# Third layer's attention: the mask added to the scores by VectorE on the way to SBUF, in place of a 16-bit product with a diagonal matrix

## The reference

```python
q = einsum('btd,dnh->btnh', layernorm(x), Wq) + bq
k = einsum('bsd,dnh->bsnh', ctx, Wk) + bk
v = einsum('bsd,dnh->bsnh', ctx, Wv) + bv
scores = einsum('bsnh,btnh->bnts', k, q) * (1.0 / sqrt(64.0))
adder = (1.0 - attention_mask[:, None, :, :]) * -10000.0
probs = softmax(scores + adder, axis=-1)
x = x + tanh(g_xattn[2]) * (einsum('bnts,bsnh->btnh', probs, v) @ Wo + bo)
```

## Time and profile before

| | |
|---|---|
| time, median of 3 runs | 1793.32 us (1789.34 to 1793.98) |
| the profiled execution's own time | 1796.88 us |
| its span, first to last instruction | 1795.2 us |
| mean granted TensorE clock over the span | 0.872 |
| busy over the span | PE 1370.8 us (76%), DVE 975.7 (54%), ACT 686.4 (38%), POOL 361.9 (20%) |
| this attention's loop, about | 719 to 1062 us of the span |

### The profile page before, as it was taken

One profiled execution on the slowest core, in us unless ns is written; L12 is line 12 of the kernel. 1 busy time (PEld: TensorE's weight loads), 2 busy tenths in 40 slices (PEclk: granted clock), 3 DMA queues, 4 the chain that ended last, 5 costly groups with the idle time before them and its releaser, 6 DMA issues. The chain is left out here.

```text
span 1795.2 us, 32731 instructions
## 1 busy us (share of the span) xinstructions
PE 1370.8 (76%) x10700; PEld 1157.7 (64%) x10709; DVE 975.7 (54%) x2389; ACT 686.4 (38%) x1370; POOL 361.9 (20%) x452
## 2 busy tenths in 40 slices
PE   4999657749599993999999989999999951102554
PEld 3777535649599982788888878799999840102232
DVE  3777654627512215555555547423223736988786
ACT  2555443510244431333333333355554252302454
POOL 1000000001122210222222222366665300001000
PEclk9999967869599996999999988799999986556787
DMA  3000020770211106111111010122223324020001
GB/s 95 19 18 13 11 76 1 231 218 1 76 40 38 38 21 210 45 45 44 48 47 51 8 58 26 42 91 92 92 90 109 141 62 109 9 56 1 1 0 47
DMA packets 96891, 108.63 MB, mean 61 GB/s; under 512 B 27888, under 2 KB 83952, under 8 KB 96496
## 3 DMA queue, kind: packets, MB, share of 16 engines
q1 hardware_dynamic: 83168, 77.77, 14.4%
q0 software_dynamic: 9984, 27.28, 4.9%
q10 hardware_dynamic: 3664, 2.63, 0.5%
HBM read 85.55 MB, written 20.97 MB: 59 GB/s over the span
## 5 line engine op out<-in xcount | busy, mean ns | idle before, releaser
L3474 PEld LDWEIGHTS L2f_bank<-L2f_xT,L2f_w_tile 128*128 128x128 f32 x1280 | 156.1, 193 | 7.5 <-ACT L2f_xT L3534 3.5
L3474 PE MATMUL L2f_bank<-L2f_xT,L2f_w_tile 128*128 128x128 f32 x1280 | 156.9, 276 | 3.0 <-ACT L2f_xT L3534 3.0
L759 POOL TENSOR_TENSOR L2x_probs<-L2x_probs,L2x_inv_sum 128x512 f32<-128x512 f32 x64 | 65.2, 1040 | 289.4 <-DVE L2x_inv_sum L1026 289.4
L3583 DVE TENSOR_TENSOR L2f_hT<-L2f_gate_h,L2f_bank 128x256 f32<-128x256 f32 x80 | 33.7, 421 | 151.9 <-ACT L2f_gate_h L3541 151.9
L3528 ACT COPY L2f_w_tile<-L2f_w_up 128x1024 f32 x80 | 83.7, 1046 | 34.8 <-issue 34.8
L3474 PEld LDWEIGHTS L1f_bank<-L1f_xT,L1f_w_tile 128*128 128x128 f32 x768 | 90.7, 194 | 1.1
L3474 PE MATMUL L1f_bank<-L1f_xT,L1f_w_tile 128*128 128x128 f32 x768 | 90.9, 277 | 0.0
L3399 POOL DMA_INDIRECT L2f_y_rows<-L2f_xn,L2f_put_row x80 | 79.0, 987 | 56.2 <-DVE L2f_xn L3599 52.7
L3391 POOL DMA_INDIRECT L2f_rows<-L2f_x_rows,L2f_take_row x80 | 77.8, 972 | 45.3 <-DVE L2f_take_row L3374 21.6
L1008 DVE TENSOR_REDUCE L2x_top<-L2x_bank 128x4 f32<-128x512 f32 x64 | 43.9, 686 | 78.8 <-PE L2x_bank L828 78.8
L3491 PE MATMUL L1f_bank<-L1f_w_down,L1f_hT 128*128 x384 | 86.7, 379 | 0.0
(11 more groups left out here) (649 smaller groups left out, 3340.5 us busy)
## 6 DMA issues: line engine op xcount, KB each, us to landing
L1f_w_up<-in_L_ffn_w SPq DMA_DIRECT2D x16, 512.0 KB, 9.6
L1f_w_down<-in_L_ffn_w SPq DMA_DIRECT2D x16, 512.0 KB, 9.0
L2f_got<-L2f_y_rows SPq DMA_DIRECT2D x16, 512.0 KB, 4.1
L2f_w_up<-in_L_ffn_gate_w SPq DMA_DIRECT2D x16, 256.0 KB, 2.8
L2f_w_up<-in_L_ffn_up_w SPq DMA_DIRECT2D x16, 256.0 KB, 2.9
L2f_w_down<-in_L_ffn_down_w SPq DMA_DIRECT2D x16, 256.0 KB, 3.6
x<-in_x SPq DMA_DIRECT2D x4, 512.0 KB, 7.6
L0x_ctx<-in_ctx SPq DMA_DIRECT2D x16, 128.0 KB, 2.1
```

The source lines that it names most:

```text
L759: nc.gpsimd.tensor_tensor(probs[c][:, :, :], probs[c][:, :, :], inv_sum[:, c, :][:, :, None].to_broadcast([P, 4, P]), ALU.mult).then_inc(s ...
L3474: x = nc.tensor.matmul(products(j, m), w_tile[j][:, at:at + P], xT[j][:, k * P:(k + 1) * P], start=(k == 0), stop=(k == KT - 1))
L3583: nc.vector.tensor_tensor(hT[j][:, 0:F], gate_h[j][:, 0:F], bank[2 + j][:, F:2 * F], ALU.mult).then_inc(q["h"], 1)
```

## The change

The pair of 16-bit products, the diagonal matrix and its preparation on GpSimd are gone. TensorE's score products no longer accumulate on anything. `shift` first computes `mask_add * 100 + scores` for each of the two banks, on VectorE with one `scalar_tensor_tensor` from PSUM to `shifted[c]`; the maximum and the subtraction then read `shifted[c]` in SBUF, the subtraction in place. TensorE's `scores` waits for a new semaphore, `masked`, which counts those operations, instead of `shifted` and `mask_add`; VectorE waits for `mask_add`, which it makes itself. The values are the same: `mask_add` is 0 or -800, exact in bf16.

```diff
@@ block.gpsimd
-            nc.gpsimd.memset(mask_diag[:, :], 0.0).then_inc(s["diag"], 1)
-            pool.wait_ge(s["diag"], 1)
-            nc.gpsimd.affine_select(out=mask_diag[:, :], ...
@@ block.tensor
             def scores(j, b, r):
-                if r == 0:
-                    pe.wait_ge(s["mask_add"], b + 1)
                 evicted(pe, b, fills.index(f"K{r}"))
-                for c in range(2):
-                    after(pe, s["shifted"], b * 4 + (2 * r + c) - 1)
-                    nc.tensor.matmul(score_bank[c][:, :].rearrange("p (h k) -> p h k", h=4), mask_diag[:, :],
-                                     mask_add[j][:, None, :].to_broadcast([P, 4, P]), start=True, stop=False)
+                after(pe, s["masked"], b * 4 + 2 * r)
                 for i in range(4):
                     for c in range(2):
                         rows = slice(64 * c, 64 * c + 64)
                         last = nc.tensor.matmul(score_bank[c][:, i * P:(i + 1) * P], qT[j][rows, 4 * r + i, :],
-                                                kT[j][rows, 4 * r + i, :], start=False, stop=(i == 3))
+                                                kT[j][rows, 4 * r + i, :], start=True, stop=True)
...
-            pe.wait_ge(s["diag"], 2)
@@ block.vector
-            def shift(b, r):
+            def shift(j, b, r):
+                if r == 0:
+                    dve.wait_ge(s["mask_add"], b + 1)
                 for c in range(2):
                     n = b * 4 + (2 * r + c)
-                    src = score_bank[c][:, :].rearrange("p (h k) -> p h k", h=4)
                     dve.wait_ge(s["scores"], n + 1)
-                    nc.vector.tensor_reduce(top[:, c, :], src, AX.X, ALU.max).then_inc(s["maxed"], 1)
+                    after(dve, s["exped"], n - 1)
+                    nc.vector.scalar_tensor_tensor(shifted[c][:, :, :],
+                                                   mask_add[j][:, None, :].to_broadcast([P, 4, P]), L2_MASK["diag"],
+                                                   score_bank[c][:, :].rearrange("p (h k) -> p h k", h=4),
+                                                   ALU.mult, ALU.add).then_inc(s["masked"], 1)
+                for c in range(2):
+                    n = b * 4 + (2 * r + c)
+                    dve.wait_ge(s["masked"], n + 1)
+                    nc.vector.tensor_reduce(top[:, c, :], shifted[c][:, :, :], AX.X, ALU.max).then_inc(s["maxed"], 1)
                     dve.wait_ge(s["maxed"], n + 1)
-                    after(dve, s["exped"], n - 1)
-                    nc.vector.tensor_tensor(shifted[c][:, :, :], src,
+                    nc.vector.tensor_tensor(shifted[c][:, :, :], shifted[c][:, :, :],
                                             top[:, c, :][:, :, None].to_broadcast([P, 4, P]), ALU.subtract
                                             ).then_inc(s["shifted"], 1)
```

More of the change, by code:

```diff
@@ L670, in wide_attention @@
         bv_wo = [sb(f"{tag}_bv_wo{i}", [P, D]) for i in range(2)]
-        mask_diag = sb(f"{tag}_mask_diag", [P, P], BF16)
         temps = sb(f"{tag}_temps", [P, 4, B])
@@ L690, in wide_attention @@
         s = core.sems_in(tag, NORM_SEMS + [
-            "w_q", "w_k", "w_v", "w_o", "biases", "diag", "ctx_in0", "ctx_in1", "mask_in0", "mask_in1", "mask_add", "xn",
-            "filled", "evicted_act", "evicted_dve", "scores", "maxed", "shifted", "exped", "summed", "inv", "scaled",
+            "w_q", "w_k", "w_v", "w_o", "biases", "ctx_in0", "ctx_in1", "mask_in0", "mask_in1", "mask_add", "xn",
+            "filled", "evicted_act", "evicted_dve", "scores", "masked", "maxed", "shifted", "exped", "summed", "inv", "scaled",
             "pT", "pT_out", "pv", "headsT", "projected", "updated", "passed",
@@ L746, in _ @@
         def _(pool):
-            nc.gpsimd.memset(mask_diag[:, :], 0.0).then_inc(s["diag"], 1)
-            pool.wait_ge(s["diag"], 1)
-            nc.gpsimd.affine_select(out=mask_diag[:, :], in_=mask_diag[:, :], compare_op=ALU.not_equal,
-                                    fill=L2_MASK["diag"], base=0, pattern=[[-1, P]],
-                                    channel_multiplier=1).then_inc(s["diag"], 1)
             def scale_rows(b, r):
@@ L1058, in body @@
             def body(j, b, first, last):
-                shift(b, 1)
+                shift(j, b, 1)
                 sums(b, 1)
@@ L1065, in body @@
                     take(1 - j, b + 1, 2)
-                    shift(b + 1, 0)
+                    shift(1 - j, b + 1, 0)
                     sums(b + 1, 0)
@@ L1079, in _ @@
             take(0, 0, 2)
-            shift(0, 0)
+            shift(0, 0, 0)
             sums(0, 0)
```

## The result

| | before | changed |
|---|---|---|
| time, median | 1793.29 us (1789.34 to 1793.98, 4 runs) | 1780.21 us (1779.45 to 1780.90, 4 runs) |
| ratio, 95% interval | | 0.9931 (0.9914 to 0.9949) |
| span of the profiled execution | 1795.2 us | 1779.2 us |
| attention stage, start of the first Q0 fill to the end of the last statistics of its x | 362.9 us | 349.9 us |
| one batch of the loop | 22.01 us | 21.15 us |

The kernel is faster by 13.1 us; 11.0 were forecast (1782.3, range 1777 to 1788). The two profiled spans differ by 16.0 us, but 2.7 of that lie ahead of the stage (the first Q0 fill starts at 699.47 and 696.73), where the change touches nothing.

A forecast was written before the change was run, and what follows sets the result against it. TensorE's full queue was taken to bound the third layer's attention. 13.2 us for removed pairs, less 0.7, 1.1 and 0.4, gave 11.0 us saved, from 1793.3 to 1782.3 us, range 1777 to 1788.

The forecast's parts named there:

- The likeliest case: Third layer's attention: removed pairs shorten TensorE's full queue, giving 1782.3 us; chance 0.73.
- pairs that leave TensorE's queue: Ahead of each `scores` call: 31 pairs of 16-bit products at 0.427 us each, 13.2 us saved.
- stall of the V1 fill in the loop: Tight half: a later Q1 eviction makes the V1 fill wait 0.05 us in 15 batches, 0.7 us lost.
- last batch: Last batch: nothing covers VectorE's longer chain, so the last weighting starts 1.1 us later.
- lead-in: Ahead of the loop: VectorE's two masks only partly covered, 0.4 us lost, bounds 0 and 1.3.
- half-size step: Ahead of the score products: 0.10 us on entering half-size tiles, expected to stay when the pair goes.
- the rival in which it goes: Score products: the half-size step leaves too, 0.53 us a pair, 14.9 us saved, 1778.4 us; chance 0.08.
- 20.9 to 21.0 us per batch: Sign in the attention loop: the batch time expected instead of 22.0 us if the forecast held.
- VectorE becomes the bound: Tight half: dearer masks and self-waits make Q1 late by 0.3 to 0.4 us a batch, 1786 to 1788; chance 0.10.
- SBUF in place of PSUM: Maxima and subtractions in `shift`: prices left unchanged, against an estimated 0.26 us saved per `shift` by the skill's page.
- The block between VectorE and GpSimd: Tight half: subtractions with two SBUF inputs and GpSimd exclude each other, 1.0 us a batch, 1797 us; chance 0.04.
- Nothing comes through: Whole kernel: the gain is lost in the clock or behind the layer, 1793 us; chance 0.05.

The follow-up runs named there:

- spare_half0: Changed kernel with one more 128x512 VectorE operation, its result unread, in `shift` of half 0: 1787.73 us, ratio 0.9960 to the kernel before, 21.68 us a batch.
- after: The changed kernel itself in its first measurement and profile, against the kernel before: 1780.21 us, ratio 0.9931.
- after_again: The changed kernel once more, unchanged, on another chip: 1814.54 us, ratio 0.9940 to the kernel before on that chip.
- after_third: The changed kernel a third time, unchanged, on another chip: 1782.54 us, ratio 0.9934 to the kernel before on that chip.
- pool_after: Changed kernel with two added GpSimd operations beside VectorE's subtractions in half 0: 1796.10 us, ratio 1.0008 to the kernel before.
- half1_dve: Changed kernel with VectorE masking only half 1, half 0 keeping the product pair: 1821.74 us, ratio 0.9985 to the kernel before on that chip.
- ends_product: Changed kernel with the product pair put back for the very first and very last scores: 1815.49 us, ratio 0.9948 to the kernel before on that chip.
- pool_before: Kernel before with two added GpSimd operations in half 0, started after the first maximum: 1795.65 us, ratio 1.0002 to the kernel before.
- product_twice: Kernel before with each product pair issued twice: 1809.34 us, ratio 1.0078 to the kernel before, 22.87 us a batch.
- spare_half1: Changed kernel with one more 128x512 VectorE operation, its result unread, in `shift` of half 1: 1782.84 us, ratio 0.9931 to the kernel before.
- tail_bias: Changed kernel with the pair back for the last scores and the bias product moved behind batch 1's T fill: 1783.86 us, ratio 0.9937 to the kernel before.

## Why the prediction was right

The likeliest case of the forecast came, and each term of its sum can be read from a row. Its mechanism explains 11.8 us of the profiled gain; the other 1.6 are a clock term that the sum lacked, and nothing that it foresaw. The terms, against the 13.4 us of the pieces:

| term | forecast | measured |
|---|---|---|
| pairs that leave TensorE's queue | 13.2 | 13.3 (30 x 0.427, and 0.53 for the pair behind the bias product) |
| stall of the V1 fill in the loop | -0.7 | 0 |
| last batch | -1.1 | -1.0 |
| lead-in | -0.4 | -0.5 |
| TensorE's clock behind the bias product | none | +1.6 |
| sum | 11.0 | 13.4 |

*The pair and the half-size step.* Both right: 0.43 a pair is shown by taking it out and by doubling it, and the step of 0.09 us in the changed kernel speaks against the rival in which it goes. The sign "20.9 to 21.0 us per batch" was a slip: by the prediction's own terms it is 22.01 - 2 x 0.427 + 0.05 = 21.2, and 21.15 was measured.

*The V1 stall* was mis-sized: 0.05 us a batch were put in, and none are there. The chain was estimated 0.18 us too long. A reduction and its subtraction were taken 0.81 us apart at first, as in the earlier trace rows; from SBUF they are 0.71 (812.16 to 812.87). The second exponential starts at 814.92, 0.04 behind its subtraction, where 0.11 was taken. With smaller differences both ways, the Q1 eviction starts 5.51 us behind the first mask instead of 5.69. So the fill that was to be 0.09 us late has 0.08 to spare, as spare_half0 found; that the added VectorE time just uses up the slack was right to 0.2 us. So the rival "VectorE becomes the bound" needed only one more operation here. The masks were at the lower bound, 684 ns. VectorE's busy time rose by 37 us (975.7 to 1012.8) and not by 44: that was 64 x 0.684, but neighbours overlap and stand 0.61 apart.

*SBUF in place of PSUM.* Leaving the moved operations at their old price was right. The maximum went from 686 to 678 ns and the subtraction from 692 to 691. The Trainium skill, "VectorE: DVE Perf Modes", section on the TRN2 errata, gives a PSUM source 120 fixed cycles and an SBUF source 58, by which each would be some 65 ns cheaper, an estimate. These rows don't show it, and the measurement decides.

*The last batch* took 1.02 us more, by the chain that was laid out. *The lead-in* lost the forecast amount, but elsewhere: up to the bias product nothing (0.04), as its end is set by VectorE's bias rows, and then 0.45 at the transposes of (0, 1), which wait for the later probabilities (1.47 us from their start to the scores, where 1.02 is the rule in the loop).

*What was missed* is the clock. The prediction used the loop's 1.00 and read nothing from the first rows behind the earlier trace rows, although the score products there had a length of 1.85 instead of 1.16. It is no sure part of the gain: after, after_again and after_third all have it, but in three other kernels with the same pause the clock was lowered (below). In a median it can't be told apart from the rest.

*The rivals.* The block between VectorE and GpSimd is real. With the added operations of pool_after it costs 0.95 us a batch, and it was kept away only by the order: GpSimd starts its scaling behind the reciprocals, 0.9 us after the last subtraction. "Nothing comes through" fell with the loop's 21.15 us a batch in three profiles of the changed kernel and its ratio of 0.993 to 0.994 in all three measurements.

## What to carry to other kernels

Work that leaves the bounding engine's queue is worth its start-to-start distance, not its span; here the 0.09 us step at the change of tile size stayed. What is added to another engine is free only up to the slack ahead of the next buffer's release: lay out that chain from starts in the trace, and test it by one spare operation. Moving a VectorE input from PSUM to SBUF bought next to nothing in time here (1 and 8 ns) and made the operation open to being blocked by GpSimd, so look for what GpSimd does at that moment.

## What the runs showed of the hardware

**TensorE's clock after a pause.** The granted level of the rows behind the bias product can be read from the length of their score products: 1.16 us at the higher level, 1.61 to 2.08 where it was lowered. With a pause of 2.97 us ahead (before, half1_dve, ends_product, pool_before, product_twice) it was lowered in 5 of 5 profiles. With 2.57 it was in 3 of 8 (spare_half0, spare_half1, pool_after). Two of these three, spare_half0 and pool_after, had also waited 0.80 and 0.78 us ahead of the K1 fill some 7 us earlier, where the other six waited 0.20. From the bias product to the next Q0 fill it took 3.73 us in the changed kernel, 5.29 without the pair's 0.53 in before, and 6.16 in half1_dve. The lower level lasted some 3.4 us in before, spare_half0 and pool_after, and some 6.8 us in the five others. What decides between the 3 and the 5 is open, and so is whether the pause or something that goes with it is the cause: tail_bias, which shortened it to 0.89 us, had the drop a little later, behind its next waits.

**In the last batch** the lower level came in 2 of 7 profiles with the longer VectorE chain, and in none of 7 without it, and made the last weighting and projection 3 us longer. That is three times what the chain itself costs. Two in seven is too few to say that the chain is the cause.
